# One set of value products per step in the first and the last batch, in place of two sets in every other step

## What is computed

```python
q = _split_heads(x @ Wq.T + bq)          # 16 heads of 16
k = _split_heads(x @ Wk.T + bk)
v = _split_heads(x @ Wv.T + bv)
scores = jnp.einsum('hbnd,hbmd->hbnm', k, q) * SCALE
attn = jax.nn.softmax(scores, axis=-1)
out = jnp.einsum('hbnm,hbmd->hbnd', attn, v)   # then out @ Wo.T + bo
x = _layernorm(x + attention)
h = jax.nn.silu(x @ wg.T) * (x @ wu.T)   # hidden size 768
x = _layernorm(x + h @ wd.T)
```

## Time and profile before

| what | value |
|---|---|
| median of 3 runs | 2720.08 us (2719.48 to 2722.92) |
| the profiled execution | 2718.36 us, span of its instructions 2716.3 us |
| busy share of the span | PE 96%, ACT 78%, DVE 47%, POOL 20% |
| batch 0's steps, 54.7 to 202.0 us | PE 125.59, ACT 124.58, DVE 42.85 us busy of 147.30 |
| batch 1, 204.5 to 368.4 us | PE 161.54, ACT 133.32, DVE 77.12 us busy of 163.90 |
| batch 15's steps, 2497.5 to 2655.2 us | PE 144.72, ACT 128.54, DVE 64.91 us busy of 157.70 |
| the tail, 2655.2 to 2716.3 us | PE 46.76, ACT 7.18, DVE 48.58 us busy of 61.10 |

### The profile page before, as it was taken

One profiled execution on the slowest core, in us unless ns is written; L12 is line 12 of the kernel. 1 busy time (PEld: TensorE's weight loads), 2 busy tenths in 40 slices (PEclk: granted clock), 3 DMA queues, 4 the chain that ended last, 5 costly groups with the idle time before them and its releaser, 6 DMA issues. The chain is left out here.

```text
span 2716.3 us, 47000 instructions
## 1 busy us (share of the span) xinstructions
PE 2606.4 (96%) x17294; PEld 936.0 (34%) x17294; DVE 1285.6 (47%) x2812; ACT 2131.7 (78%) x2370; POOL 538.6 (20%) x542
## 2 busy tenths in 40 slices
PE   6879999999999999999999999999999999999897
PEld 2223333333324333333333323333333333334234
DVE  3324445454453544445454553545445454453447
ACT  2878878788787878878788787878878788787781
POOL 2101122121222212122121121212122121221113
PEclk9999999999999999999999999999999999999998
DMA  4112021120212102121120202102121030201000
GB/s 154 49 39 70 26 79 38 48 71 22 87 34 74 48 22 86 33 75 41 30 85 25 87 29 73 55 14 94 33 75 40 22 95 25 87 29 56 18 27 29
DMA packets 81742, 144.08 MB, mean 53 GB/s; under 512 B 27584, under 2 KB 29504, under 8 KB 79424
## 3 DMA queue, kind: packets, MB, share of 16 engines
q1 hardware_dynamic: 79968, 139.81, 16.5%
q10 hardware_dynamic: 1504, 0.66, 0.1%
HBM read 88.48 MB, written 50.33 MB: 51 GB/s over the span
## 5 line engine op out<-in xcount | busy, mean ns | idle before, releaser
L599 ACT ACTIVATE probs<-psum 128x1024 f32<-128x1024 f32 x2048 | 1983.7, 1023 | 497.3 <-PE psum L1010 497.1
L1010 PE MATMUL psum<-probs,v 128*32 128x512 f32 x8192 | 1007.2, 610 | 39.9 <-DVE flipped L850 39.3
L1010 PE MATMUL psum<-kstack,qstack 51*128 51x512 f16 x4096 | 633.4, 384 | 31.9 <-ACT probs L599 28.0
L1010 PEld LDWEIGHTS psum<-probs,v 128*32 128x32 f32 x8192 | 217.3, 110 | 555.0 <-issue 522.1
L1010 PEld LDWEIGHTS psum<-kstack,qstack 51*128 51x128 f16 x4096 | 134.3, 93 | 724.0 <-ACT probs L599 647.2
L510 POOL TENSOR_TENSOR ffn<-h,ffn 128x512 f16<-128x512 f32 x192 | 221.4, 1155 | 678.1 <-DVE ffn L769 578.5
L724 DVE SCALAR_TENSOR_TENSOR tanh_out<-tanh_out,psum 128x512 f32<-128x512 f32 x192 | 131.3, 684 | 335.4 <-ACT tanh_out L580 335.4
L715 DVE SCALAR_TENSOR_TENSOR parts<-psum,scales,parts 128x512 f16<-128x512 f32 x128 | 94.9, 741 | 269.1 <-ACT parts L571 268.9
L489 POOL TENSOR_TENSOR squares<-parts 128x512 bf16<-128x512 f16 x128 | 131.9, 1038 | 433.0 <-DVE parts L715 433.0
L503 POOL TENSOR_TENSOR rstd<-vareps,minus_half 128x2 f32<-128x2 f32 x128 | 89.6, 700 | 584.3 <-DVE vareps L788 584.3
L1010 PE MATMUL psum<-ffn,gateT 128*128 128x512 f16 x768 | 200.4, 384 | 0.3 <-DVE ffn L757 0.3
(11 more groups left out here) (102 smaller groups left out, 1529.9 us busy)
## 6 DMA issues: line engine op xcount, KB each, us to landing
parts_dram<-parts SPq DMA_DIRECT2D x64, 512.0 KB, 2.8
qstack<-parts_dram SPq DMA_DIRECT2D x384, 64.0 KB, 2.1
kstack<-parts_dram SPq DMA_DIRECT2D x384, 64.0 KB, 2.1
x_pre<-in_x_t SPq DMA_DIRECT2D x17, 1024.0 KB, 5.1
x_res<-in_L_attn_x SPq DMA_DIRECT2D x16, 1024.0 KB, 5.2
out<-x_res SPq DMA_DIRECT2D x32, 512.0 KB, 2.7
kstack<-shift_parts SPq DMA_DIRECT2D x384, 4.0 KB, 1.7
ffn<-in_L_ffn_w_gate SPq DMA_DIRECT2D x1, 768.0 KB, 9.7
```

Of the source, the lines that this page charges most:

```text
L599: nc.scalar.activation(probs[:, (STEPS * b + k) % SLOTS, 2 * pr:2 * pr + 2, :], scores[pr], ACT.Exp, scale=score_scale[par]).then_inc(prob ...
L1010: return nc.tensor.matmul(o, lhsT, rhs, start=start, stop=stop)
```

## The change

In batch 0 and in batch 15 each step issues one set of value products, P(k-2), instead of two sets in every even step. In batch 15 the last two products of batch 14 stand in steps 0 and 1. The 14 batches between keep the pairs.

```diff
                     score(b, k, first)
                     if k == RELOAD and not last:
                         pe.reg_load(general, flag[0:1, 0:1])
-                    if k % 2 == 0:
+                    if first or last:
+                        if k >= 2:
+                            products(b, par, k - 2, first)
+                        elif last:
+                            products(b - 1, 1 - par, STEPS + k - 2, False)
+                    elif k % 2 == 0:
                         for earlier in (k - 2, k - 1):
                             if k:
                                 products(b, par, earlier, first)
-                            elif not first:
+                            else:
                                 products(b - 1, 1 - par, STEPS + earlier, False)
```

## The result

| what | before | with the change |
|---|---|---|
| median of 9 runs each | 2719.93 us (2717.31 to 2722.92) | 2728.05 us (2725.12 to 2733.14) |
| the profiled execution | 2718.36 us, span 2716.3 us | 2727.24 us, span 2725.2 us |

The ratio is 1.0037 (1.0028 to 1.0047, 95%): the change makes the kernel 0.37% slower, 8.1 us, where 2728.0 was predicted. All distances inside a batch are counted from its first exponential, E(0,0).

A forecast was written before the change was run, and what follows sets the result against it. In batches 0 and 15 neither TensorE nor ScalarE is full; a loop of waits sets each pair. Batch 0's 0.0 and batch 15's +7.7 turn 2718.36 into 2726.0; the median, 1.7 above, gives 2728 us, range 2722 to 2732.

The forecast's parts named there:

- The loop, and the term of 3.72 plus the piece: Batches 0 and 15: a pair of steps costs 3.72 us plus its piece, which was free before; empty pairs take 3.77.
- Batch 0 at 0.0: Batch 0: losses in pairs with a piece and gains in empty steps and at the ends sum to 0.0 us.
- the 1.7 us of half clock: Batch 0's steps: the stretch at 1.2 GHz stays after the change and costs the same 1.7 us.
- P(8) starts at 2526.05 as before: Batch 15, step 10: P(8) still waits for VectorE's copy of ACC; E(12,0) behind it comes 2.6 us earlier.
- The rival of a clock that falls at the standstill: Batch 15 at P(8), or a 1.2 GHz stretch in fuller odd steps: +2.6 or +1.7, then 2730.5; chance 0.15.
- The wait of 2.1: Batch 15 at P(8): TensorE waits 2.1 us instead of 4.35, and the clock is assumed to stay at 2.4 GHz.
- Gate and up, down: Batch 15: twelve gate and up pairs 5.55 against 4.79, +9.1 us; eight half-down pairs 5.14 against 4.57, +4.6.
- The residual is ready at 2666.2: End of batch 15: drain, normalise, store, reload and bias take over; the value products lead only to 2664.8.
- the end at +7.7: Batch 15 to the tail's first out drain: 2666.3 against 2658.66, +7.7 us.
- Cheaper changeovers: Batches 0 and 15: the piece follows the set at 0.88 instead of 0.98; -4.7, so +3.0, 2723; chance 0.19.
- The wait isn't there: Odd steps' S(k,1) never waits, TensorE's work sets the pair: batch 0 -15, batch 15 -7.5, 2697; chance 0.08.

The follow-up runs named there:

- number 5: The change, with the piece ahead of the set in odd steps of batches 0 and 15; 2729.89 us against 2718.28 before, ratio 1.0044.
- number 9: As number 4, with hi in batch 0 moved between the next step's two exponentials; 2701.09 us against 2715.13 before, ratio 0.9953.
- number 1: The change kept in batch 0 only, batch 15 as before; 2721.66 us against 2721.24 before, ratio 1.0005.
- number 2: The change kept in batch 15 only, batch 0 as before; 2733.19 us, ratio 1.0053 to the kernel before.
- number 8: The change in batch 15 only, run once more unedited; 2724.38 us against 2715.13 before, ratio 1.0029.
- number 6: The change, with POOL's bias of the last batch over one of 8 tiles; 2726.35 us, ratio 1.0028 to the kernel before.
- number 7: The change itself, run once more unedited; 2725.81 us against 2715.13 before, ratio 1.0044.
- number 10: As number 9, with batch 15's residual loaded early into an idle buffer and given its bias there; 2701.80 us, ratio 0.9946 to the kernel before.
- number 4: The change, with the single set between a step's two scores, in all of batch 0 and short steps of batch 15; 2710.68 us, ratio 0.9960 to before.
- number 3: The change, with single sets only in pairs of steps whose piece is small, in batches 0 and 15; 2712.75 us, ratio 0.9973 to the kernel before.

## Why the prediction was right

**The loop, and the term of 3.72 plus the piece: right.** Predicted and measured pairs: 4.78 and 4.80 (half qk, two units of v), 5.04 and 5.06 (hi), 5.55 and 5.58 (gate and up), 5.14 and 5.16 (down), 4.25 and 4.33 (x1T), 3.77 and 3.74 (empty). For x1T the piece was mis-sized: 0.66 less the overhang of 0.07 is 0.59, not 0.53, and 0.58 is what the trace has (2528.31 to 2528.89). Number 5 reordered what lies in the loop and left it as long; number 9 took the wait out of it, and the length fell to TensorE's own work.

**Batch 0 at 0.0: right in sum** (-0.25), with number 1's time in agreement, but two of its terms were off and cancel. The prediction kept the 1.7 us of half clock among the steps. In the three profiled executions with batch 0 as before (before, 2, 8) a stretch lies at 178.6 to 178.9, where TensorE waits 0.91 and 0.53 us in each empty pair; in the five with the change's batch 0 (the change, 1, 5, 6, 7) none lies among the steps. E(0,0) to E(63,0) takes 145.04, where 199.2 less 54.71 is 144.5 without the stretch and 146.2 with it. What makes it up is the way into batch 1, put at no difference: from E(63,0) to the next first exponential it takes 4.56, before 3.68, and 4.5 to 4.7 in the other four. Why is open; the profile shows nothing that TensorE waits for there. That the sum came out at nothing is luck in these 0.9 us.

**"P(8) starts at 2526.05 as before": wrong.** The step took the time of VectorE's copy from one execution as fixed. It hangs on the reload of x_res, and that isn't fixed. These are the times of batch 15, relative to E(0,0), in all twelve executions, the change's last:

| profiled execution | reload, issue to bias | bias starts | P(8) | its wait |
|---|---|---|---|---|
| before | 7.82 | 13.90 | 28.54 | 4.35 |
| number 10 | 7.80 | 13.89 | 28.51 | 4.69 |
| number 4 | 7.70 | 13.80 | 28.43 | 4.61 |
| number 6 | 7.18 | 13.26 | 27.89 | 1.30 |
| number 7 (the change) | 6.99 | 13.08 | 27.70 | 1.12 |
| number 1 | 6.98 | 13.06 | 27.68 | 1.84 |
| number 9 | 6.90 | 12.99 | 27.62 | 3.80 |
| number 5 | 6.69 | 12.78 | 27.39 | 0.80 |
| number 3 | 6.69 | 12.79 | 27.42 | 3.62 |
| number 2 | 6.24 | 12.33 | 26.94 | 0.36 |
| number 8 (as number 2) | 5.98 | 12.07 | 26.69 | 0.11 |
| the change | 5.70 | 11.78 | 26.51 | none |

P(8) starts 14.6 behind the bias in every row with a wait, so the chain from the reload was read rightly; the transfer took between 5.7 and 7.8. With the change TensorE itself arrives at 26.5, as the prediction's 2524.0 said (2524.0 less 2497.51), so it waits for what the reload takes beyond some 5.8 (26.5 less 14.6, less the 6.1 at which it is issued). E(12,0) came 3.85 earlier than before in place of 2.6. Why the transfer varies is open; number 7, which is the same program, had 6.99. Numbers 3, 4, 9 and 10 keep the pairs beside out, arrive at 23.8, and still wait (3.62 to 4.69); number 1, behind a stretch of half clock at 2509.0, arrives at 25.8.

**The rival of a clock that falls at the standstill** didn't come: in the profiled execution TensorE didn't stand there at all, and the clock over 2521.7 to 2526.0 stayed at 1.00. Nor did it fall there in numbers 2, 5, 6, 7 and 8, with waits of 0.11 to 1.30; in the five executions with waits of 3.62 to 4.69 (before, 3, 4, 9, 10) it did. The wait of 2.1 that the prediction reckoned with came in none, so its choice there wasn't tested.

**Gate and up, down: right,** +0.5 us in all on 108 us. With x1T's +0.2 and the standstill's -1.25 that puts S(58,0) at 151.5 behind E(0,0) where 152.0 was predicted.

**"The residual is ready at 2666.2", the end at +7.7: mechanism right, size short by 1.9.** VectorE waited for POOL's bias and not for TensorE, as said. But the way from S(58,0) to the end of the bias took 17.62, 1.0 more than the 16.65 reckoned, and that 1.0 is the reload: from its issue to the bias 5.74, before 4.75, and between 4.67 and 6.02 in the eleven executions that have it. And a step was missing: the prediction let the value products' own chain go on while the bias ran. L860 is held until the bias ends, and L864 behind it, so that the drain comes 1.0 behind the residual. Number 6 shows that the bias does it. The Trainium skill ("SBUF — State Buffer", the section on who interferes with whom) states that a VectorE instruction with two inputs in SBUF contends with a GpSimd instruction that reads SBUF. The rows agree: of the chain's steps under the bias, the reciprocal took 0.25 as without it, and L860, with both inputs in SBUF, took 3.69 in place of 0.42.

**What the sum left at nothing and wasn't:** the start (-1.1), the end of the tail (-1.1) and the middle batches (+2.4), in all of which the program is unchanged. They are spread: over the twelve executions the first exponential comes between 53.15 and 54.89 (53.47 to 54.89 in those with the change's batch 0), and the tail from its first out drain on takes between 56.3 and 57.6 in the eleven that leave it as it is (numbers 5 and 6 have 57.6 and 57.5). The last section takes the middle batches apart. These, the standstill and the end miss by +1.2 in the profiled execution; the median is within 0.1 of the forecast, which is partly luck, since runs of one kernel differ by 5.6 and 8.0 us in the table at the top and by up to 18.7 beside numbers 7 to 10.

**"Cheaper changeovers": refuted.** The piece follows the set at 1.00, not at 0.88 (64.77 to 65.77), and its weights are loaded when it starts (65.76), not ahead.

**"The wait isn't there": not in the change** (the wait of 0.52 in each odd step), but its arithmetic describes number 9, which removes that wait by order alone: 4.24 where it had 4.1. So the prediction's reason against it, that two score buffers don't allow it, was wrong: they do, once the set stands between the two scores.

## What to carry to other kernels

Before a matmul is moved, look for the point at which TensorE's order waits for another engine: work ahead of that wait is free up to its length, work behind it is in the loop. Here the same set of products costs 0.18 to 0.8 us a pair behind the second score, where the piece is longer than 0.88, and gains 0.37 ahead of it (4.60 to 4.23, pairs with half a qk and no hi). What is gained in a stretch is not all kept: of the 14.0 us that number 9 takes out of batch 0's steps, 3.3 come back at the wait ahead of batch 1. And a wait on a chain with a transfer in it should be taken from more than one execution, or given its spread.

## What the runs showed of the hardware

**A standstill and a stretch of half clock in each middle batch.** TensorE is busy without a break for 142.8 us of a middle batch. Then, in step 58, P(56) waits for VectorE's copy of ACC, and a stretch of half clock follows. Batch 2 with the change, in the timeline and in a view of the stretches:

```profile
513.63 2.75 PE L1010 MATMUL psum<-probs,v 128*32 128x512 f32 x16 [2.53 <-DVE flipped L850]
```

```profile
511.10:513.60 2.50, 0.00 (x0) 0.00 (x1) 2.27 (x9) 1.76 (x2) 0.00 (x0) 1.00 0.00 0
514.60:518.00 3.40, 3.40 (x20) 0.71 (x12) 2.67 (x4) 1.04 (x2) 0.00 (x0) 0.50 0.06 11
```

The copy stands in VectorE's order behind a normalisation that waits for POOL's rstd (L503): P(56) starts 4.29 to 4.31 us behind the start of that rstd in all 168 middle batches of the 12 profiled executions. The standstill is in all of them too, and takes 1.79 to 4.17 us. The clock of 0.50 begins within 4 us of its start in 156 of them and lasts 3.4 us, in 12 of these 6.8; in the other 12 it doesn't fall, with waits of 1.79 to 3.30. So the wait comes first, but its length alone doesn't decide, and what does is not settled. (In 7 executions another stretch begins in the first microseconds of batch 1 or reaches into them.)

Without half clock (12 batches) a middle batch takes 159.67 us and its standstill, to within 0.01. With one stretch of 3.4 us it is 161.25 and its standstill (160.94 to 161.37), so the stretch costs 1.6. In sum the 14 middle batches took between 2289.1 and 2300.3 us, which is more than the whole effect of the change. In before and after they differ by 2.4: the standstills sum to 34.9 and 36.1, which is 1.2, and the stretch at 204.0, with its 1.6, covers the rest. A difference of some 2 us in such a kernel is found in the distances of one trace, not in its time.

**VectorE behind GpSimd, to the end of its instruction.** In 14 places of the twelve executions L860 runs into POOL's bias (L523, 4.5 us), in batch 1 or in the tail. It takes 1.74 to 4.14 us, whatever the bias leaves, and ends 0.28 or 0.29 behind the bias in all 14. With number 3 it ran 3.41 us to 2647.29, the bias to 2647.01; with number 9 1.95 us to 2640.57, the bias to 2640.29. With nothing of POOL beside it, it takes 0.42 or 0.43, and beside POOL's squares (L489, 1.04 us) mostly 0.78. In number 10 the normalisation of x_res (L808 there, one SBUF input beside per-row scalars, two instructions) took 4.94 from 2633.11 on, in place of some 0.74, while the bias ran from 2633.03 to 2637.57. There it held up nothing on the path.
